# Decoder layer on one core: quarter-tile products and a two-bank projection in self-attention, unfused values in cross-attention

## The reference

```python
x = layernorm(x + self_attn(x))    # causal, 16 heads of 64; q per head, ONE k and ONE v for all heads
x = layernorm(x + cross_attn(x, ctx))  # 16 heads of 64, q from x, k and v per head from ctx (width 96), + bo
x = layernorm(x + ffn(x))          # 8 experts, top 2 of them per token, silu(a) * b, hidden 256
# self_attn: xn = layernorm(x)*g1; q, k = l2norm(xn@Wq.T), l2norm(xn@Wk.T); p = softmax(mask(16*q@k.T))
#            out = layernorm(concat_heads(p@v) @ Wout.T) * g2
# cross_attn: p = softmax(q@k.T/8) over the 64 context rows of the same sequence;
#            out = concat_heads(p@v) @ Wo + bo
```

## Time and profile before

| | |
|---|---|
| median of 3 runs | 885.01 us (880.82 to 885.24) |
| profiled execution, whole time | 882.52 us |
| its span, first to last instruction | 880.8 us |
| mean granted PE clock | 0.981 of full speed |
| busy in the span | PE 89%, DVE 72%, ACT 67%, POOL 51% |

### The profile page before, as it was taken

The page is one execution under the profiler, slowest core; times in us unless marked ns, Lnnn a source line. Parts: engine busy times, 40 slices in busy tenths (PEclk is TensorE's granted clock), DMA queues, the critical chain, the costliest instruction groups (busy, mean ns, idle before and its releaser), DMA issues.

```text
span 880.8 us, 26463 instructions
## 1 busy us (share of the span) xinstructions
PE 783.5 (89%) x9205; PEld 654.3 (74%) x9237; DVE 632.1 (72%) x1898; ACT 593.7 (67%) x1444; POOL 452.0 (51%) x440
## 2 busy tenths in 40 slices
PE   4799999999999988999999999999997877687776
PEld 3577777778787767888888878788886767677752
DVE  3878778878787757778787878788888555445425
ACT  2677878888787856777676767777766454455535
POOL 5477676776767632223535353535342545554443
PEclk9899999999999999999999999999999999889998
DMA  8499999000000000000000000000002455556636
GB/s 282 82 157 161 158 156 121 2 0 0 0 0 0 2 1 6 7 7 7 27 10 28 10 28 9 24 13 25 12 22 73 136 166 175 159 177 184 204 104 231
DMA packets 69505, 65.30 MB, mean 74 GB/s; under 512 B 5689, under 2 KB 54972, under 8 KB 69280
## 3 DMA queue, kind: packets, MB, share of 16 engines
q1 hardware_dynamic: 62592, 51.42, 28.5%
q0 software_dynamic: 4736, 10.12, 3.3%
q10 hardware_dynamic: 2080, 2.49, 0.9%
HBM read 35.88 MB, written 28.58 MB: 73 GB/s over the span
## 4 chain that ended last, share of the span: by engine, by line
PE 51%; issue 20%; POOL 12%; ACT 6%; DVE 6%; DMA 3%; another core or an unknown queue 1%; SPq 1%; POOLq 0%; ACTq 0%; DVEq 0%
PE bank L1791 7%; PE bank L1687 7%; PE bank L1487 6%; PE bank L1489 5%; PE bank L1488 5%; POOL rq L530 5%; PE bank L1662 3%; PE bank L1675 3%; POOL PR L535 3%; PE bank L1801 3%; PE bank L1563 2%; PE bank L1571 2%; ACT VBD L391 2%; PE bank L1781 1%; POOL rs L544 1%
## 5 line engine op out<-in xcount | busy, mean ns | idle before, releaser
L391 ACT COPY VBD<-bank 64x512 f32<-64x512 f32 x192 | 111.2, 579 | 28.5 <-PE bank L1489 25.8
L567 POOL TENSOR_TENSOR PR<-PR,rL 128x1024 f32<-128x1024 f32 x32 | 60.9, 1902 | 115.7 <-DVE rL L1114 115.6
L530 POOL TENSOR_TENSOR rq<-ssq,mhalf 128x17 f32<-128x17 f32 x32 | 99.2, 3100 | 15.7 <-DVE ssq L963 15.1
L627 POOL DMA_INDIRECT zbuf<-PT,KT x71 | 69.8, 983 | 72.3 <-ACT PT L889 50.2
L535 POOL TENSOR_TENSOR PR<-PR,rL 128x1024 f32<-128x1024 f32 x32 | 60.9, 1904 | 82.4 <-DVE rL L994 82.4
L1417 DVE SCALAR_TENSOR_TENSOR stage<-bank,b_now,early 128x128 f32<-128x128 f32 x142 | 43.1, 345 | 61.9 <-ACT early L881 46.2
L1791 PE MATMUL bank<-xT,w_now 128*128 128x128 f32 x568 | 82.7, 292 | 0.4 <-DMA w_now<-in_wl 0.3
L619 POOL DMA_INDIRECT xbuf<-xg,slot x64 | 64.9, 1014 | 34.3 <-DVE xg L1283 21.8
L881 ACT ACTIVATE early<-bank,b_now 128x128 f32<-128x128 f32 x142 | 44.4, 367 | 56.3 <-PE bank L1791 38.4
L1791 PEld LDWEIGHTS bank<-xT,w_now 128*128 128x128 f32 x568 | 73.8, 203 | 1.6 <-issue 1.3
L797 ACT ACTIVATE PT<-bank 128x512 f32<-128x512 f32 x64 | 38.3, 600 | 43.3 <-PE bank L1675 41.5
(11 more groups left out here) (243 smaller groups left out, 2338.8 us busy)
## 6 DMA issues: line engine op xcount, KB each, us to landing
w_now<-in_wl SPq DMA_DIRECT2D x71, 256.0 KB
xbuf<-blank SPq DMA_DIRECT2D x1, 17160.0 KB, 120.5
KT<-xbuf SPq DMA_DIRECT2D x71, 65.0 KB
VBD<-zbuf SPq DMA_DIRECT2D x4, 512.0 KB, 5.1
out<-X SPq DMA_DIRECT2D x8, 256.0 KB, 2.3
cT<-in_ctxT ACTq DMA_DIRECT2D x16, 96.0 KB, 2.0
zbuf<-PT,KT POOLq DMA_INDIRECT x71
wl_sb<-in_wl POOLq DMA_DIRECT2D x1, 1024.0 KB, 9.3
```

The lines of the kernel that those rows point to most:

```text
L391: u = copy(VBD[h * SEQ:(h + 1) * SEQ, p, s, lo:lo + blocks, :], bank[CHUNK_BANK[c]][s * SEQ:(s + 1) * SEQ, :].rearrange("k (a d) -> k a d" ...
L530: nc.gpsimd.tensor_tensor(rq[:, :], ssq[:, :], mhalf[:, 0:HEADS + 1], ALU.pow).then_inc(a["pow"], 1)
L567: nc.gpsimd.tensor_tensor(v, v, rL[:, p, :].unsqueeze(2).broadcast_to([P, HEADS, SEQ]), ALU.mult)\
L627: nc.gpsimd.indirect_dma_start(out=zbuf, out_offset=at, in_=yb[:, t % YB, :], in_offset=None, bounds_check=K2 * TOK - 1, oob_is_err=False) ...
```

## The change

Four things are altered. (1) Self-attention: the mask product is split into four quarter tiles of the PE array (64 rows by 64 columns), `values` uses a plain copy of v on both halves of the partitions and becomes four quarter-tile products 512 columns wide; because of where these put the heads, `project` becomes 32 quarter-tile products that accumulate in two banks (0 and 1), with a second copy of Wout whose halves are swapped, and DVE adds the two banks (`y_take`). The v part of `qkv` is computed by four products of 128 rows by 64 columns, so that each half of the partitions holds it; `v_bd` goes, ACT's `v_keep` copies vS instead. (2) Cross-attention: Wv·Wo is no longer formed; `b_v` makes plain values (two chunks of 512 columns per tile instead of four), `b_o` multiplies them by the weights (32 quarter-tile products), `b_oT` copies the result out (bank 4 on ACT, bank 5 on DVE), and `b_y` projects it with Wo by 32 quarter-tile products into banks 1 and 5. (3) The bias bo is added to X beforehand on POOL (`add_bo`), and DVE adds two banks to it. (4) Stages change places in the cross steps, on PE, ACT, DVE and POOL. Core of the diff:

```diff
 # PE, self-attention
+                if not isinstance(t, int):            # in x_T
+                    pe.wait_ge(a["kvS"], t)
+                    pe.wait_ge(a["oT"], 2 * (t - 3))
+                    pe.wait_ge(a["yS"], t - 4)
...
-                M(bank[1][:, 0:2 * DH], xT[:, p, :], wkv_sb[:, :], start=True, stop=True).then_inc(a["kv"], 1)
+                M(bank[1][:, 0:DH], xT[:, p, :], wkv_sb[:, 0:DH], start=True, stop=True)
+                for s in range(PB):
+                    for h in range(2):
+                        m = M(bank[1][h * DH:(h + 1) * DH, (1 + s) * DH:(2 + s) * DH], xT[:, p, s * SEQ:(s + 1) * SEQ],
+                              wkv_sb[:, DH:2 * DH], start=True, stop=True)
...
                 for h in range(2):
-                    M(bank[6 + h][:, :], ident_b[:, :], causal[:, :, :].rearrange("q h k -> q (h k)"), start=True, stop=False)
+                    r = slice(h * DH, (h + 1) * DH)
+                    for s in range(PB):
+                        M(bank[6 + h][s * SEQ:(s + 1) * SEQ, :], ident_b[r, r],
+                          causal[r, :, :].rearrange("q h k -> q (h k)"), start=True, stop=False)
...
-                M(bank[4 + s][:, :], VBD[:, p, s, 0, :], PT[:, s * HW:(s + 1) * HW], start=True, stop=True)\
+                for s in range(PB):
+                    for h in range(2):
+                        r = slice(h * DH, (h + 1) * DH)
+                        half = s if h == 0 else 1 - s
+                        m = M(bank[4 + h][half * DH:(half + 1) * DH, :], vS[r, p, s, :], PT[r, s * HW:(s + 1) * HW],
+                              start=True, stop=True)
...
                 for k in range(NBLK):
-                    m = M(bank[0][:, 0:D], OT[:, k, :], wout_sb[:, k, :], start=(k == 0), stop=(k == NBLK - 1))
+                    g = dict(start=(k == 0), stop=(k == NBLK - 1))
+                    M(bank[0][0:SEQ, 0:D], OT[lo, k, even], wout_sb[lo, k, :], **g)
+                    m0 = M(bank[0][SEQ:P, 0:D], OT[lo, k, odd], wout_swap[lo, k, :], **g)
+                    M(bank[1][0:SEQ, 2 * D:3 * D], OT[hi, k, odd], wout_sb[hi, k, :], **g)
+                    m1 = M(bank[1][SEQ:P, 2 * D:3 * D], OT[hi, k, even], wout_swap[hi, k, :], **g)
 # DVE, self-attention
+            def y_take(t, p):
+                dve.wait_ge(a["yA"], t + 1)
+                V.tensor_tensor(yS[:, :], bank[1][:, 2 * D:3 * D], yA[:, :], ALU.add).then_inc(a["yS"], 1)
...
                 stage_of(sums, i, p, 0)
+                stage_of(y_take, i, p, 3)
                 stage_of(ln_var, i, p, -2)
...
-                stage_of(v_bd, i, p, 1)
 # PE, cross-attention
+            def b_o(t, p):
+                pe.wait_ge(b["pT"], 2 * (t + 1))
+                for k in range(NBLK):
+                    for h in range(2):
+                        r = slice(h * DH, (h + 1) * DH)
+                        for s in range(PB):
+                            half = s if h == 0 else 1 - s
+                            m = M(bank[4 + h][half * DH:(half + 1) * DH, k * SEQ:(k + 1) * SEQ], VBD[r, p, s, k, 0:DH],
+                                  PT[r, k * P + s * SEQ:k * P + (s + 1) * SEQ], start=True, stop=True)
+            def b_y(t, p):
+                for h in range(2):
+                    pe.wait_ge(b[f"oT{h}"], t + 1)
+                for k in range(NBLK):
+                    M(bank[1][0:SEQ, 0:D], OT[lo, k, even], xwo_sb[lo, k, :], **g)   # and three more, to banks 1, 5, 5
...
+                if fresh:                                # fresh: odd step, pair: even step
+                    b_v(i - 1, 0)
                 stage_of(lambda t, q: b_pT(t, q, 1), i, p, 2)
+                if pair:
+                    b_q(i, 2)
+                    b_q(i, 3)
+                if fresh:
+                    b_v(i - 1, 1)
+                stage_of(b_o, i, p, 2)
+                if pair:
+                    b_k(i, 0)
+                    b_k(i, 1)
+                if fresh:
+                    b_v(i - 1, 2)
                 stage_of(b_y, i, p, 2)
+                if pair:
+                    b_k(i, 2)
+                    b_k(i, 3)
+                if fresh:
+                    b_v(i - 1, 3)
 # DVE, cross-attention
+                if fresh:
+                    b_v(V.tensor_copy, dve, i - 1, 1)
+                stage_of(b_sum, i, p, 1)
+                stage_of(lambda t, q: b_oT(V.tensor_copy, dve, t, 1), i, p, 2)
                 if pair:
                     b_k(V.tensor_copy, dve, i, 1)
+                stage_of(b_add_y, i, p, 2)
+                stage_of(b_stats, i, p, 2)
+                if pair:
                     b_k(V.tensor_copy, dve, i, 3)
```

More of the change, by code:

```diff
@@ L583, in cross @@
                     sends = (0, 1)
[L584 removed]
                 if sends:
                     send(g, sends[0])
[L587 removed]
+                stage_of(b_weights, i, p, 1)
                 if sends:
                     send(g, sends[1])
[L590 removed]
+                stage_of(cross_tail, i, p, 2)
                 if len(sends) > 2:
@@ L800, in cross @@
                 pair = p == 0 and has(i)
+                fresh = p == 1 and has(i)
                 if pair:
@@ L812, in cross @@
                     b_q(i, 1)
-                if p == 1 and has(i):
-                    b_u(nc.scalar.copy, act, i - 1, 0, 0)
+                if fresh:
+                    b_v(nc.scalar.copy, act, i - 1, 0)
                 stage_of(lambda t, q: b_pT(t, q, 1), i, p, 2)
@@ L979, in normalise @@
                      .then_inc(a["qn"], 1)
-            def v_bd(t, p):
-                dve.wait_ge(a["vS"], t + 1)
-                if later(t, 2):
-                    dve.wait_ge(a["o"], 2 * (t - 1))
-                for h in range(2):
-                    v = V.tensor_copy(VBD[h * DH:(h + 1) * DH, p, 0, 0, h * DH:(h + 1) * DH], vS[0:SEQ, p, :])
-                v.then_inc(a["v0"], 1)
             def softmax(t, p):
@@ L1574, in _ @@
-            pe.wait_ge(consts, 11)
-            def vo_product():
-                pe.wait_ge(w_vo, 32)
-                for c in range(NVO):
-                    r = slice(c % 2 * DH, (c % 2 + 1) * DH)
-                    for k in range(HVO):
-                        blk = 2 * k + c // 2
-                        m = M(bank[4 + c][0:CD, k * D:(k + 1) * D], xwvT_sb[r, blk, :], xwo_sb[r, blk, :],
-                              start=True, stop=True)
-                    m.then_inc(b["vo"], 1)
+                pe.wait_ge(a["vS"], t + 1)
@@ L1730, in cross @@
                     slot_tile(-1, -1 % JB)
-                if p == 0 and has(i):
+                pair = p == 0 and has(i)
+                fresh = p == 1 and has(i)
+                if pair:
                     b_q(i, 0)
@@ L1755, in cross @@
                     route_places(g)
-                if p == 1 and has(i):
-                    for c in range(NVO):
-                        b_uv(i, 1, c)
+                if pair:
+                    b_k(i, 2)
+                    b_k(i, 3)
+                if fresh:
+                    b_v(i - 1, 3)
                 if isinstance(i, int) and i == 0:
@@ L1763, in cross @@
                     project(T - 2, 0)
-                    for c in range(2):
-                        values(T - 1, 1, c)
+                    values(T - 1, 1)
                     project(T - 1, 1)
-            pe.wait_ge(a["kn"], T)
+            pe.wait_ge(a["kvS"], T)
+            pe.wait_ge(a["yS"], T - 3)
             bx_T(0, 0)
```

281 lines of the change are left out of this document (137 added, 144 removed).

## The result

The changed kernel takes 984.78 us (median of 4 runs, 982.85 to 989.61) against 884.87 us: 1.1149 times as long, 95% interval 1.1094 to 1.1204. It is slower, as forecast, but by 100 us and not by 50. The profiled execution has a span of 987.8 us against 880.8.

The account below looks back on a forecast made before the run. A ring of POOL and DVE, not PE, was taken to set the self-attention step, PE's work plus waits cross-attention. Forecast: 882.5 + 14 (self-attention) - 3 (start) + 40 (cross-attention) = 933 us, range 908 to 957.

Parts of the forecast that it names:

- a second ring in self-attention: Self-attention: q, projection, ACT's copy, DVE's addition to rinv and back to q would set the step, 9.6 against 9.08, +14 us.
- new waits in cross-attention: Cross-attention: three new waits of PE would lengthen four tiles from 44.4 to 49.7 us, +40 us in all.
- plus 1.0: Cross-attention, per four tiles: DVE's router work delays the maxima and no longer has slack behind it, 1.0 us (0 to 2).
- the wait for yA, none for rq, PE's gap before q: Self-attention signs in the profile after: DVE waits for yA at `y_take`, no longer for rq at rinv; PE idles before q.
- Rival (a): Self-attention: the ring through the projection has more slack, DVE's saved copies show, 8.7 per step, 908 us in all; chance 0.13.
- Four quarters at once: Self-attention projection: quarter-tile products run four at once, 16 rounds at 0.109 us, plus 0.1 us per step.
- Rival (e): Projections: quarter products with 128 columns overlap only in twos, 1.7 us for each of 64, about 1040 us; chance 0.04.
- PE's own work in cross-attention: Cross-attention: PE's products without router go from 19.7 to 19.4 us per pair of tiles, nothing gained.
- PT before `b_o`: Cross-attention, odd steps: PE waits 1.3 us for ACT's copy of the second half of PT.
- OT before `b_y`: Cross-attention, odd steps: PE waits 1.2 us for DVE's copy into OT, behind value chunk 1 and the softmax sum.
- KT before the scores: Cross-attention, every second step: PE waits 0.85 us for DVE's copy of key chunk 3, which `b_y` covered before.
- The expert layer is unchanged and starts later: Behind cross-attention: the expert layer was taken as unchanged, only starting later, with no term of its own in the sum.

Follow-up runs that it names:

- e7: The changed kernel with the blank transfer started at step 10 and DVE's addition of the two projection banks moved behind two other operations; 951.1 us.
- e9: e8 and e7 together, with the router's picks and ACT's exponential moved behind the score maxima of the next cross-attention step; 904.3 us.
- e5: The changed kernel with ACT copying the second half of PT ahead of value chunk 0 in odd cross-attention steps; 1001.3 us.
- e8: e3 with three cross-attention orders changed: OT copied first of all on DVE, PT ahead of value chunk 0, key chunks 2 and 3 before `b_y`; 940.1 us.
- e4: The changed kernel with DVE's copy into OT (`b_oT`) ahead of the softmax sum in cross-attention; 967.2 us.
- e2: The kernel before with the cross-attention part of the change alone; 956.9 us.
- e3: The changed kernel with the 17 MB blank transfer for xbuf started at step 10 of self-attention; 964.8 us.
- e1: The kernel before with the self-attention part of the change alone; 930.7 us.
- e6: The changed kernel with key chunks 2 and 3 multiplied and copied before `b_y` in even cross-attention steps; 972.5 us.

## Why the direction was right and the time wrong

The direction and the two mechanisms (a second ring in self-attention, new waits in cross-attention) were right. The time is not: 984.8 us lies outside 908 to 957. Two steps failed. The waits of cross-attention, added one by one with "plus 1.0" for DVE's router work, were priced too low, and what they do to the clock was left out: +40 us forecast, +69 measured. And the supply of PE's instructions was not priced at all: 22 us. Step by step:

**The self-attention ring.** Right in every sign that was named: the wait for yA, none for rq, PE's gap before q. The size was 9.33 instead of 9.6: +7 us, not +14. In the step from 241.58 to 251.04 the terms are 3.42 from q to the projection (counted 2.93 + 0.6), 2.15 to ACT's copy (2.16), 0.40 to the addition (0.34), 2.45 to rinv (2.57) and 1.04 to q (1.05), in all 9.46, and 9.19 in the next: the new shapes of the v products and DVE's small operations were each priced 0.1 too high. e7 shows the cause directly: move the one instruction and the step falls from 9.33 to 8.86. Rival (a)'s premise, 8.7 per step, is what the stage gives then.

**Four quarters at once.** Right: 32 projection products take 1.9 us, 0.11 per round of four. Rival (e) is refuted.

**PE's own work in cross-attention,** 19.7 to 19.4 per pair, "nothing gained". In e9, with the clock up as in before, the rest is 7.2 us less for eight pairs: 0.9 a pair, three times the forecast. It did not matter beside the waits.

**The waits of cross-attention, the step that failed first.** "Pair 22.8, four tiles 45.6, plus waits of the router and its work 3.1 as before, plus 1.0": 49.7, and measured 55.3 (16 tiles in 221.1 us). That is 10.3 over before's 45.0, not 5.3. Per four tiles, forecast and measured (a quarter of the table above): PT before `b_o` 2.6 and 1.8; OT before `b_y` 2.4 and 3.9, because odd steps pay 1.56 instead of 1.2 and half of the even ones 0.75; KT before the scores 1.7 and 3.1, because the copy's wait is 1.2 to 1.3 instead of 0.85 and half of the odd steps wait as well (0.56), for the addition that frees bank 5; transposes 1.0 and 2.1. In all idle 12.7, where 7.7 and before's share were counted. "1.0 (0 to 2)" for DVE's router work was the wrong kind of term: the four waits share one engine's order, so that each delay of DVE is passed to the next. e5 shows the circle (one wait shortened by 4.7 us, the next longer by 3.8), e8 and e9 the router's part in it (24 us of the stage, some 4 of them the clock's).

**The clock, not in the sum at all.** Cross-attention of before ran at 2.4 GHz, all but its last us. After has 31 us of it at 1.2 GHz; each such stretch begins at most 3.1 us after a gap of 1.5 us or more. The reverse does not hold: most gaps as long are not followed by one, and in e4 two stretches begin with no such gap in the 34 us before them. What decides stays open. Where the clock is down, a round of the projection takes 0.215 us instead of 0.11; PE's timeline at full and at half clock:

```profile
437.81 0.27 PE L1718 MATMUL bank<-xwo_sb,arena 64*64 64x128 f32 x1
...
437.92 0.27 PE L1718 MATMUL bank<-xwo_sb,arena 64*64 64x128 f32 x1
...
547.18 0.42 PE L1718 MATMUL bank<-xwo_sb,arena 64*64 64x128 f32 x1
...
547.39 0.42 PE L1718 MATMUL bank<-xwo_sb,arena 64*64 64x128 f32 x1
```

What it costs is best read where the code is the same. After, e2, e3 and e7 share their cross-attention. Of its groups of four tiles from the 11th softmax sum on, nine ran wholly at full clock and took 54.1 us, two with 3.4 us at the lower clock took 54.8, five with 6.8 us took 55.7 to 55.8: some 0.24 us lost for each us at the lower clock. So about 5 of the 41 us that these 16 tiles lost are the clock's, and by the same rate (an estimate from these groups) 7 of the stage's 69; at full clock throughout, four tiles would still take 54.1 instead of 49.7. PE's idle time thus has a second, smaller price. The Trainium skill (TensorE: Matmul & The Clock Gate, HAM oscillation) says that waits between bursts bring the clock down again; the stretches of after agree with that, those two of e4 do not show it.

**Instructions, the step that was missing.** The prediction asks of each product whether it lies behind a wait or costs time; of the instructions it never asks. The first steps of self-attention, unrolled, and the loop's first pass take packets every 6.5 us on the average when nothing is in their way (e3), and get one every 9.6 beside a transfer that fills every DMA engine: 22 us.

**The end.** "The expert layer is unchanged and starts later" leaves out that its first tiles stand between the last cross steps. Counted from the last softmax sum, the activation of its tile 3 comes at 11.7 us before and at 20.2 after (11.8 in e1, 16.5 to 21.1 in all kernels with the new cross-attention); from there on both take the same within 1 us. What orders these last steps was not tested.

Put together: forecast -3 + 14 + 40 = 51 for the execution; measured 107 = -1 start, +7 ring, +22 instructions, +69 cross-attention (instead of 40; about 7 of it the clock's), +9 end, +1 between.

**Left open:** what orders the first ten and the last three tiles of cross-attention in e9, where 14 of its remaining 19 us lie; why the packets come further apart in e1 than in after, which accounts for some 8 of its 10.5 us of further stalls; and what brings the clock down behind one gap and not behind the next.

## What to carry to other kernels

Work saved on the busiest engine of a pipelined kernel brings nothing while a ring of copies and hand-overs sets the step, so first find the first instruction behind each hand-over and ask what stands ahead of it on its engine: three small moves (e4, e6, e7) were worth 12 to 18 us each. Waits in one engine's order must be costed as one chain, not added up: shortening one alone bought nothing, and the stage grew by 8 us with the clock (e5). And when products get smaller and more numerous, count the instructions as a transfer of their own, and keep bulk transfers out of the stretches that fetch them. To see how much order is left to gain, look at the ends of a stage apart from its middle: in e9 the middle is nearly right and the ends are not.

## What was not expected of the hardware

- Instruction packets of 16 KB took 1.3 to 1.5 us each beside the bulk transfer and 0.9 to 1.7 elsewhere (after), hardly a difference. What the transfer changed is how soon one follows another: 9.0 us or more from start to start beside it, 3.8 to 8.1 without it (e3). PE stood up to 4.9 us for one.
- Once the loop of self-attention has been passed once, no packet starts on q8 (none from 132 to 317 us in after). Its first pass still fetches: two of the nine gaps, 3.2 us, lie there (115.65 and 124.62 us).
- At full clock the products of 128 rows by 64 columns for v, with a weight load each into the same rows, ran as four rounds in 0.39 us, entry and exit included.
